# Taking the self loops out of the edge list of a three-layer graph convolution

## What is computed

```python
src, dst, norm = _gcn_norm(edge_index, n)        # appends a self loop for every node, once more
# deg = number of edges into a node; norm = dinv[src] * dinv[dst], dinv = rsqrt(deg)
def _gcn_conv(x, W, b, src, dst, norm, n_nodes):
    xw = x @ W
    msg = xw[src] * norm[:, None]
    out = jax.ops.segment_sum(msg, dst, num_segments=n_nodes)
    return out + b
h = _gcn_conv(x, W1, b1, ...); h = _gcn_conv(h, W2, b2, ...); h = _gcn_conv(h, W3, b3, ...)
x = _layernorm(x + h)
```

## Time and profile before

| | us |
|---|---|
| median of 3 runs | 3293.23 (3293.22 to 3293.64) |
| the profiled execution | 3293.62 |
| its span, first to last instruction | 3291.8 |
| PE busy | 2606.0 |
| POOL busy | 2360.8 |
| DVE busy | 1123.5 |
| ACT busy | 155.8 |

### The profile page before, as it was taken

The page is one execution under the profiler, slowest core; times in us unless marked ns, Lnnn a source line. Parts: engine busy times, 40 slices in busy tenths (PEclk is TensorE's granted clock), DMA queues, the critical chain, the costliest instruction groups (busy, mean ns, idle before and its releaser), DMA issues.

```text
span 3291.8 us, 21460 instructions
## 1 busy us (share of the span) xinstructions
PE 2606.0 (79%) x6574; PEld 1095.5 (33%) x6574; DVE 1123.5 (34%) x2036; ACT 155.8 (5%) x272; POOL 2360.8 (72%) x2511
## 2 busy tenths in 40 slices
PE   7798899989998967777877777776777777777876
PEld 5333333333333323233332323332232222322332
DVE  7233223322332323233222333232434443444434
ACT  1000000000000000000000000000000000000000
POOL 0577777777777657777777777766777777777775
PEclk9999999999999989999999999998999999999998
DMA  7777777777777657777777777766777777777776
GB/s 287 224 223 222 220 223 224 225 220 223 223 223 220 207 160 223 223 221 225 223 223 220 223 223 223 220 205 206 236 229 235 236 236 236 233 238 235 235 229 187
DMA packets 243773, 736.07 MB, mean 224 GB/s; under 512 B 43286, under 2 KB 44946, under 8 KB 243664
## 3 DMA queue, kind: packets, MB, share of 16 engines
q0 software_dynamic: 199440, 653.68, 67.9%
q1 hardware_dynamic: 44224, 81.08, 6.7%
HBM read 683.39 MB, written 51.20 MB: 223 GB/s over the span
## 4 chain that ended last, share of the span: by engine, by line
POOL 47%; issue 15%; DMA 1%; PE 1%; DVE 0%; ACT 0%; DVEq 0%; POOLq 0%
POOL ring L391 47%; PE ps L553 1%; DMA y_dram<-acc 0%; DMA ring<-y_dram,src_idx 0%; PE ps L606 0%; ACT acc L689 0%; DVE acc L899 0%; DVE h_sb L917 0%; DVE ln L926 0%; DVE h_sb L924 0%; POOLq L77 0%; DVEq L896 0%; DVE row_sb L907 0%; PE ps L601 0%; DVE h_sb L907 0%
## 5 line engine op out<-in xcount | busy, mean ns | idle before, releaser
L391 POOL DMA_INDIRECT ring<-y_dram,src_idx x2493 | 2357.8, 946 | 907.8 <-issue 757.9
L553 PE MATMUL ps<-ring,onehot 128*128 128x512 f32 x4986 | 2340.7, 618 | 645.5 <-DMA ring<-y_dram,src_idx 588.4
L553 PEld LDWEIGHTS ps<-ring,onehot 128*128 128x128 f32 x4986 | 938.2, 196 | 2012.1 <-issue 1610.8
L899 DVE SCALAR_TENSOR_TENSOR acc<-ps,mask,acc 128x512 f32 x624 | 439.6, 746 | 1262.8 <-PE ps L553 1221.7
L881 DVE TENSOR_TENSOR onehot<-ps,lo_f 128x512 f32<-128x512 f32 x624 | 427.0, 685 | 704.6 <-PE ps L553 704.6
L579 PE MATMUL ps<-w,w_sb 128*128 128x512 f32 x376 | 169.0, 592 | 0.0
L689 ACT ACTIVATE acc<-h_sb,dinv 128x512 f32<-128x512 f32 x96 | 69.2, 721 | 1389.2 <-DVE h_sb L907 1389.2
L579 PEld LDWEIGHTS ps<-w,w_sb 128*128 128x128 f32 x376 | 71.4, 190 | 89.9 <-issue 89.9
L907 DVE SCALAR_TENSOR_TENSOR h_sb<-ps,dinv,bias 128x512 f32<-128x512 f32 x48 | 36.0, 750 | 135.2 <-PE ps L579 128.9
L685 ACT ACTIVATE w_sb<-ps 128x512 f32<-128x512 f32 x47 | 28.1, 597 | 622.4 <-PE ps L563 622.4
L703 ACT ACTIVATE ln<-ln 128x1 f32<-128x1 f32 x49 | 9.9, 203 | 734.1 <-DVE ln L932 734.1
(11 more groups left out here) (109 smaller groups left out, 186.4 us busy)
## 6 DMA issues: line engine op xcount, KB each, us to landing
ring<-y_dram,src_idx POOLq DMA_INDIRECT x2493, 3.7
y_dram<-acc SPq DMA_DIRECT2D x96, 256.0 KB
acc<-in_x_dram SPq DMA_DIRECT2D x1, 12288.0 KB
y_dram<-acc SPq DMA_DIRECT2D x12, 1024.0 KB
w_sb<-in_x_dram SPq DMA_DIRECT2D x48, 256.0 KB, 4.5
out_dram<-row_sb SPq DMA_DIRECT2D x48, 256.0 KB
w_sb<-in_L_gnn_W_dram SPq DMA_DIRECT2D x1, 1024.0 KB
w<-in_L_gnn_W_dram SPq DMA_DIRECT2D x1, 1024.0 KB
```

What stands on the lines that cost most here:

```text
L391: pool.indirect_dma_start(ring[:, s, :], None, y_dram[layer], bass.IndirectOffsetOnAxis(ap=rows, axis=0)).then_inc(done, 16)
L553: mm = pe.matmul(ps[:, g % BANKS, :], onehot[:, r, k, :], ring[:, r * CPQ + k, :], start=(opens and k == 0), stop=(closes and k == chunks ...
L899: dve.scalar_tensor_tensor(out=rows, in0=ps[:, g % BANKS, :], scalar=mask[:, part, own:own + 1], in1=rows, op0=ALU.mult, op1=ALU.add).then ...
```

## The change

The self loops that stand in the list are taken out of it on the chip, and the resident row in `acc` counts for both loops of its node. 100,000 edges are left, which is 782 chunks and 49 steps a layer, with lag 2 throughout. The last quad of a layer has 2 chunks.

- **Shares.** Each partition p also loads a contiguous share of the lists, 912 (`LINE`) entries of `dst` (913) and `src` from entry 832p on (`near_dst`, `near_src`), in four DMAs. The `src` list in the turned form isn't loaded on this path.
- **Packing.** DVE packs source, place and tile difference into one word (`pack_ids`, `pack_moves`), zeroes the words of the loops (`drop_ends`) and closes the holes with six masked shifts by 1, 2, 4, 8, 16 and 32 places (`pick_moving`, `move_left`). This is spread over the gaps between the eight batches of counting; shifts 1 to 5 come after dinv. The last one raises `packed_ready`.
- **Lines.** From the first node of each share, DVE and PE work out where in the packed store each line of 128 edges begins (`owner`, `line_idx`; 14 products of one column). POOL stores the packed words to `lines_dram`, waits for that, and gathers 14 times up to 128 pieces of 64 words (`gather_lines`). DVE and PE unpack and turn them (`keep_lines`, `turn_lines`) into `src_idx`, `lo_f` and `group_tile`.
- **Order of the start.** x is scaled on ACT (`scale_x`), four tiles and then one weight copy in turn. SP stores three pieces of y0, waits for `packed_ready`, loads W1 (its place in SBUF served the packing), and stores the rest. The W1 turns and products of PE stand around `turn_lines`. The first gather waits for `src_ready`, `groups_ready` and the stores.
- **Factors.** The masks are 0.5 or 0 and the scale after a layer is `dinv_sum` = 2 dinv, so the row in `acc` counts twice.

The core of the diff:

```diff
@@ sync: loads and y0 stores
+            def load_near(near, edges, width):
+                sp.dma_start(near[0:P - 1, 0:width], bass.AP(edges.tensor, 0, [[SHARE, P - 1], [1, width]])).then_inc(near_loaded, 16)
+                sp.dma_start(near[P - 1:P, 0:LAST_SHARE], ...).then_inc(near_loaded, 16)
+            load_list(dst_rows, dst, dst_loaded)
+            load_near(near_dst, dst, LINE + 1)
+            load_near(near_src, src, LINE)
...
+                for k in range(3):
+                    store_y0(k)
+                sp.wait_ge(packed_ready, 1)
+                load_w1()
+                for k in range(3, X_BATCHES):
+                    store_y0(k)
+                store_last_y0()
@@ gpsimd
                 if n == 0:
+                    pool.wait_ge(src_ready, 1)
                     pool.wait_ge(groups_ready, 1)
...
+            def gather_lines():
+                pool.wait_ge(packed_ready, 1)
+                pool.memset(lines[:, LINE_BLOCKS - 1, :], (N % P) << SRC_BITS).then_inc(line_padded, 1)
+                pool.dma_start(lines_dram.rearrange("(p e) a -> p (e a)", e=LINE), packed).then_inc(packed_stored, 16)
+                pool.wait_ge(line_padded, 1)
+                pool.wait_ge(packed_stored, 16)
+                for b in range(LINE_BLOCKS):
+                    rows = LAST_LINES if b == LINE_BLOCKS - 1 else P
+                    for h in range(PAIRS):
+                        pool.indirect_dma_start(lines[0:rows, b, h * NEAR:(h + 1) * NEAR], None, lines_dram,
+                                                bass.IndirectOffsetOnAxis(ap=line_idx[0:rows, b, h:h + 1], axis=0)
+                                                ).then_inc(lines_gathered, 16)
@@ tensor
+            pe.wait_ge(owner_ready, 1)
+            for b in range(LINE_BLOCKS * PAIRS):
+                mm = pe.matmul(ps[:, OWNER_BANK, P // 2 + b:P // 2 + b + 1], owner[:, b * P:(b + 1) * P], share[:, 3:4], ...)
...
+                for k in range(FB, 3 * FB + 4):
+                    weight_step(k)
+                turn_lines()
+                for k in range(3 * FB + 4, W_STEPS):
+                    weight_step(k)
@@ scalar
+                for k in range(X_BATCHES):
+                    for r in range(X_BATCH):
+                        scale_x(X_BATCH * k + r)
+                    copy_weights(FB + k, FB + k + 1)
+                scale_x(TILES - 1)
+                copy_weights(FB + X_BATCHES, W_STEPS)
@@ vector
+            link(dve.tensor_scalar(owner, line_from, share[:, 1:2], None, ALU.is_ge))
+            dve.scalar_tensor_tensor(out=owner, in0=line_from, scalar=share[:, 2:3], in1=owner,
+                                     op0=ALU.is_lt, op1=ALU.mult).then_inc(owner_ready, 1)
...
+            def pick_moving(k):
+                caught_up()
+                link(dve.tensor_scalar(sign, packed, BITS - 1 - k, 31, ALU.logical_shift_left, ALU.arith_shift_right))
+                mark(dve.tensor_tensor(moving, packed, sign, ALU.bitwise_and))
+            def move_left(k):
+                by = 1 << k
+                caught_up()
+                link(dve.tensor_tensor(packed, packed, moving, ALU.bitwise_xor))
+                return dve.tensor_tensor(packed[:, 0:LINE - by], packed[:, 0:LINE - by], moving[:, by:LINE], ALU.bitwise_or)
             place_batch(0, 0, True)
+            pack_ids()
             place_batch(1, 1, True)
-            with dve.Fori(1, COUNTS // 2) as m:
-                for buf in range(2):
-                    place_batch(2 * m + buf, buf, False)
+            pack_moves()
+            place_batch(2, 0, False)
+            drop_ends()
+            place_batch(3, 1, False)
+            check_loops()
+            place_batch(4, 0, False)
+            check_ends()
+            place_batch(5, 1, False)
+            pick_moving(0)
+            place_batch(6, 0, False)
+            mark(move_left(0))
+            place_batch(7, 1, False)
...
-                invert_degrees()
-                scale_x()
-                keep_edges()
+                invert_degrees(2.0)
+                for k in range(1, BITS - 1):
+                    pick_moving(k)
+                    mark(move_left(k))
+                pick_moving(BITS - 1)
+                move_left(BITS - 1).then_inc(packed_ready, 1)
+                keep_lines()
                 keep_groups()
```

More of the change, by code:

```diff
@@ L53, in gcn_three_layers_resnorm @@
     RING = RING_QUADS * CPQ
[L55 to L73, removed]
+    LAG = 2
+    LOOP_TILES = STEPS - LAG
+    CONSTS = 7
+    LINE_CONSTS = 6
+    SHARE = -(-E // P)
+    SHARE += -SHARE % NEAR
+    LAST_SHARE = E - (P - 1) * SHARE
+    MOST_ENDS = (1 << BITS) - 1
+    MOST_NEAR = LINE - SHARE - NEAR + 1
+    LINE_BLOCKS = -(-USED // P)
+    LAST_LINES = USED - (LINE_BLOCKS - 1) * P
+    PAIRS = P // NEAR
+    SRC_BITS = 13
+    LOW_BITS = SRC_BITS + 7
+    SPAN = CPG + 2
+    assert LOOP_TILES == TILES - 2 and CPS * N == EDGES
+    assert SPARE * N <= EDGES * P and E == EDGES + N and EDGES % N == 0
+    assert D == 512 and LIST_STEPS % 2 == 0 and LAST < P and TAIL_EDGES and PADS < CPQ
+    assert (TILES - 1) % X_BATCH == 0 and FULL_BLOCKS + 1 == ROW_BLOCKS == LINE_BLOCKS
+    assert LIST_GROUPS % COUNTS == 0 and COUNTS % 2 == 0 and GPB * MIDS <= 256
+    assert N <= 1 << SRC_BITS and P == 1 << 7 and SRC_BITS + 13 + BITS == 32 and 0 < LAST_SHARE < SHARE
+    assert LINE * P > EDGES
+    lines_dram = nc.dram_tensor("lines_dram", [P * LINE, 1], I32, kind="Internal").ap()
     y_dram = [nc.dram_tensor(f"y{l}_dram", [N, D], F32, kind="Internal").ap() for l in range(LAYERS)]
@@ L291, in _, with load_list @@
             tail_at = FULL_BLOCKS * P * P
[L292 to L295, removed]
+            def load_list(rows, edges, loaded):
+                r3 = rows.bitcast(I32).rearrange("c (b p) -> c b p", p=P)
                 sp.dma_start(r3[:, 0:FULL_BLOCKS, :],
@@ L748, in _ @@
                 act.wait_ge(dinv_ready, 1)
+                act.wait_ge(x_all_loaded, 32)
+                for t in range(TILES):
+                    scale_x(t)
                 for layer in range(LAYERS):
@@ new lines, in check_loops, with check_ends, check_spread @@
+            def check_loops():
+                mark(dve.tensor_tensor(near_src, near_src, here, ALU.not_equal))
+                caught_up()
+                link(dve.scalar_tensor_tensor(out=near_src, in0=near_src, scalar=-1.0, in1=ends, op0=ALU.add, op1=ALU.add))
+            def check_ends():
+                link(dve.tensor_tensor(near_src, near_src, ends, ALU.mult))
+                mark(dve.tensor_reduce(broken[:, 0:1], near_src, AX.X, ALU.max))
+            def check_spread():
+                spread = lists[:, 0:LIST_CHUNKS - SPAN]
+                link(dve.tensor_tensor(spread, used[:, SPAN:LIST_CHUNKS], used[:, 0:LIST_CHUNKS - SPAN], ALU.subtract))
+                link(dve.tensor_reduce(broken[:, 2:3], spread, AX.X, ALU.max))
@@ L907, in bias_rows @@
                 dve.scalar_tensor_tensor(out=h[:, :], in0=ps[:, bank, :] if layer == 0 else tile_of(t),
[L908 removed]
+                                         scalar=dinv_sum[:, bass.ds(t, 1)], in1=bias[:, 0, :] if layer == 0 else ps[:, BIAS_BANK, :],
                                          op0=ALU.mult, op1=ALU.add).then_inc(h_ready, 1)
@@ L916, in norm_rows @@
                     dve.wait_ge(o_ready, t)
-                dve.scalar_tensor_tensor(out=row, in0=tile_of(t), scalar=dinv[:, bass.ds(t, 1)], in1=ps[:, BIAS_BANK, :],
+                dve.scalar_tensor_tensor(out=row, in0=tile_of(t), scalar=dinv_sum[:, bass.ds(t, 1)], in1=ps[:, BIAS_BANK, :],
                                          op0=ALU.mult, op1=ALU.add).then_inc(ln_step, 1)
@@ L1006, in _ @@
                     for i in range(STEPS):
-                        step(layer, i, TILE_AT[i])
+                        step(layer, i, i - LAG if i >= LAG else None)
                     last_tiles(layer)
```

339 lines of the change are left out of this document (233 added, 106 removed).

## The result

| | before | changed |
|---|---|---|
| median, us | 3293.22 (4 runs) | 3170.24 (4 runs) |
| profiled execution, us | 3293.62 | 3174.01 |
| its span, us | 3291.8 | 3172.2 |

The ratio is 0.9629 (95% interval 0.9617 to 0.9641), 123 us less. The forecast was 3134 us with a range of 3120 to 3157: right in sign, 36 us off, and outside the range.

The account below looks back on a forecast made before the run. The prediction took POOL's gathers, one per 1.25 us, as the bound. Span 3291.8 - 183.8 (gathers) + 23.8 (start) + 1.2 (layer ends) = 3133.0 us, giving a median of 3134 us, range 3120 to 3157.

Parts of the forecast that it names:

- Gathers removed: In the three layers: 49 fewer gathers each, 147 in all, at 1.2504 us, -183.8 us.
- Layer ends: At each layer's end the last quad holds two chunks, not three: +0.4 us each, +1.2 us for three.
- (a): Start, ahead of the counting: share loads in near 8.5 us, batch 0 at 17.2 and not 14.7, +2.5 us.
- (b): Start, between counting batches: 14.2 us of DVE packing, partly filling 9.2 us of waits; batches end at 57.6 against 49.1.
- (c): Start, after dinv: five more shift rounds on DVE take 20.7 us, putting packed_ready at 91.2.
- the rival of cheap bit work: Integer operations on DVE run at the one-tensor rate, packed_ready comes 12 us earlier: 3123 us, 12% chance.
- (d): Store leg of the start: after packed_ready 11.6 MB at 380 GB/s plus 7.4 us, y0 stored at 129.1.
- (e): Line leg of the start: packed store 5.5 us, 14 line gathers landed at 118, small steps 9.7, done at 127.7.
- The rival of lines stuck behind the stores: Packed store and line gathers delayed by SP's backlog: first gather at 140 to 155, 3145 to 3160 us, 16% chance.
- (f): Behind the first gather: last W1 products make weights ready at 144, before POOL's 17th gather at 149, costing nothing.
- PE sets layer 0: A lower granted clock makes PE the bound in layer 0: about 20 us at 0.86, 3155 us, 5% chance.

Follow-up runs that it names:

- the cut at 112: The changed kernel with each of the two 127-partition share loads issued as two DMAs, rows 0 to 111 and 112 to 126: 3136.63 us, ratio to before 0.9523.
- the kernel where SP waits: The kernel with the cut at 112 and the early round, with SP holding W1 and nine y0 stores until POOL's packed store has landed: 3130.34 us, ratio 0.9505.
- the early round: The kernel with the cut at 112, with one of five shift rounds after dinv moved ahead of the list-order flag: 3132.81 us.

## Right and wrong, point by point

**Gathers removed: right.** 147 at 1.250 us. PE's load in layer 0 was 887.9 of 977.2 us, 91% where 89% was forecast, and POOL waited 0.9 us for it. **Layer ends: right** in size, +1.4 us against +1.2.

**The start, (a): wrong, and this is nearly the whole miss.** The step priced the four share loads by "0.93 MB at 386 GB/s", the rate of loads with 128 rows, and put their end at 8.5 us. It was at 43.96. The bytes were right; what failed is that a rate from one shape was taken for another. The row that could have warned is 386 GB/s as the sum of sixteen engines: 24 GB/s each, so the number of engines is the first thing to ask of a new DMA. The Trainium skill says it outright (DMA: Bandwidth & Descriptors, section Why a DMA increments its semaphore by 16 and not by 1): the DMA gets the largest number of engines up to 16 that divides the slowest dimension of both sides, and 127 partitions give one. The runs agree at 127, 124 and 126. With the loads cut at 112, they are in at 10.7, still 2.2 us after the forecast.

**(b), (c): right.** The batches ended 48.0 us after the shares were in, where 49.1 was forecast, and packed_ready came at 125.3, 81.3 after them against 82.7. A bitwise operation on two integer tensors of 912 columns took 1.11 us, as taken from the float row:

```profile
106.70 1.11 DVE L1011 TENSOR_TENSOR kept<-kept,ring 128x912 int32<-128x912 int32 x1
```

So the rival of cheap bit work falls.

**(d), (e): the wrong leg was the longer one.** From packed_ready to the first gather passed 42.5 us in the changed kernel and 42.0 with the cut at 112; the line leg had been put at 36.5 and the store leg at 37.9. The line leg was short by 6.0: the packed store took 8.9 us and not 5.5, the last lines landed 6 us after their gather's start and not 4.7, and the small steps took 11.2 and not 9.7. The store leg was close to the forecast: with the cut at 112 the engines are at their full rate until 121.5 us, at 398 to 413 GB/s and not 380, and then comes a tail to 127, 36.4 after packed_ready. What the tail is, the sum didn't ask, and it is the same matter as the share loads. The first two lines are from the kernel with the cut at 112, the other two from the kernel before, at its start and at the end of layer 0 (us, busy of each engine, clock, DMA share, GB/s):

```profile
120.00:121.00 1.00, 0.00 (x0) 0.00 (x0) 0.00 (x0) 0.00 (x0) 0.00 (x0) 0.50 1.07 410
125.00:126.00 1.00, 1.00 (x6) 0.51 (x6) 0.00 (x0) 0.00 (x0) 0.00 (x0) 0.50 0.13 51
...
102.00:103.00 1.00, 0.80 (x2) 0.00 (x0) 0.00 (x0) 0.17 (x1) 0.00 (x0) 1.00 0.13 51
1170.00:1172.00 2.00, 0.00 (x0) 0.00 (x0) 0.00 (x0) 0.00 (x0) 0.00 (x0) 0.50 0.13 48
```

51 GB/s at a share of 0.13 is two engines of sixteen. What SP stores last is the last tile, 106 rows of 2 KB (6,250 - 48 x 128), and the largest divisor of 106 up to 16 is 2; from 1167.5 to 1172.8 us the trace of the kernel before has 106 packets of 2,048 bytes. So this store takes some 5 us, inside the "7.4 for start and landing" of the sum, and POOL waits for it in the kernel before and in the kernel where SP waits. No run cut it in two, so what that would give isn't shown. The rival of lines stuck behind the stores is half right: the engines are shared, and it costs 4 to 5 us, not 11 to 26.

**(f): right**, W1's last product is copied at 183.8, 4 us before the 17th gather.

The tally for the changed kernel: shares +35.5, DVE's packing -1.4, behind packed_ready +4.7 over the 37.8 of the sum, which is the 38.8 us between 129.0 and 167.8. The median lies 3.8 us under the profiled execution, so its distance to the forecast is 36. With the cut at 112 the same terms are +2.2, -2.8 and +4.2: that this kernel ends 3 us from the forecast is in part luck, errors that cancel.

## What to carry over

Before a DMA is priced by bytes, look at its row count: 127 rows moved at 26 GB/s where 128 move at 386, 15 times slower, and a cut into 112 + 15 or 126 + 1 rows brings it back for one more issue a load, where 124 + 3 does so only in part. In a traced stretch, a DMA share of 0.06 (one engine) or 0.13 (two, the 106-row store) says this at a glance. When a change adds a round trip through HBM, send it ahead of the bulk transfers that the same event releases, in the same queue; here that was worth 4 us, and the version with it, the cut at 112 and the early round has 3128.4 us, a ratio to before of 0.950 where the changed kernel has 0.963.

## What the runs showed beside that

On one chip the kernel before took 3730.75 us and the variants 3542 to 3547, all 13% more. The granted clock was 0.86 to 0.87 over the span, not 0.96, and POOL no longer set the pace. Busy times between 300 and 400 us of layer 0, first in the changed kernel, then in the one that waits for the packed store:

```profile
300.00:400.00 100.00, 91.51 (x220) 40.18 (x220) 30.51 (x46) 6.59 (x10) 75.63 (x81) 0.98 0.76 223
```

```profile
300.00:400.00 100.00, 75.28 (x174) 33.06 (x173) 23.81 (x35) 5.27 (x8) 65.27 (x70) 0.87 0.66 192
```

81 gathers fell to 70 in 100 us, though one gather still took 946 ns. In layer 0 POOL stood 146.7 us inside the layer (34.0 put to PE, 112.7 to a releaser that the profile doesn't know), where it stood 0.9 in the changed kernel. Behind the 17th gather the kernel holds POOL inside a layer only by `summed`, which PE raises, so this is the rival "PE sets layer 0", which no run on the other chips showed. That PE is behind these waits is argued from the kernel, not shown row by row: PE's records in that trace don't fit the other engines' (none from 345.3 to 356.9 us, while DVE adds a group of its sums at 350.7). And the rival had two things wrong. It isn't layer 0 alone: from 1500 to 1600 us 70 gathers stand against 81 as well. And it isn't 20 us at a clock of 0.86 but 412 at 0.87 (3542.59 against 3130.34): its price, some 11 us for each hundredth below 0.88, doesn't hold here, and why stays open. The ratio to before hardly moved (0.949 to 0.951), which fits with PE having 49 chunks a layer less as well.
